# One transformer block on one core: the a weights get a scale of their own, and the a products of the first group run first

## The reference

```python
h = _layernorm(x) * (1 + ca) + sa                 # x: 2 x 4096 x 512
xn = h / norm(h) * sqrt(512) * gamma
q, kv, a = split(xn @ W_qkva.T, 3);  a = sigmoid(a)
y = scan: y[t] = a[t] * y[t-1] + kv[t]            # along the 4096 steps
x = x + ga * (q * y)
h = _layernorm(x) * (1 + cb) + sb                 # then an FFN, whose operands are
x = x + gb * ffn(h)                               # quantised in blocks of 16 to FP4 values
```

## Time and profile before

| | us |
|---|---|
| median of three runs | 1933.85 (1933.53 to 1935.3) |
| the profiled execution's own time | 1935.68 |
| span from its first to its last instruction | 1933.9 |
| PE busy | 1910.6 (99%) |
| DVE busy | 1683.4 (87%) |
| POOL busy | 1298.5 (67%) |
| ACT busy | 759.5 (39%) |
| mean granted TensorE clock | 0.996 |

### The profile page before, as it was taken

The page is one execution under the profiler, slowest core; times in us unless marked ns, Lnnn a source line. Parts: engine busy times, 40 slices in busy tenths (PEclk is TensorE's granted clock), DMA queues, the critical chain, the costliest instruction groups (busy, mean ns, idle before and its releaser), DMA issues.

```text
span 1933.9 us, 26907 instructions
## 1 busy us (share of the span) xinstructions
PE 1910.6 (99%) x9147; PEld 899.7 (47%) x9147; DVE 1683.4 (87%) x2106; ACT 759.5 (39%) x1013; POOL 1298.5 (67%) x1136
## 2 busy tenths in 40 slices
PE   8999999999998999999999999999999999999998
PEld 3344444444444444444444444444444444444444
DVE  7867687778779999999999999999999999999986
ACT  4566767766543233323232323232323322332321
POOL 1568778787767667667766776677667766766641
PEclk9999999999999999999999999999999999999999
DMA  8978788898953433343334333433343343334323
GB/s 292 303 172 217 183 210 207 211 215 185 203 145 90 94 89 73 78 92 86 73 81 96 79 74 84 96 79 74 87 96 73 73 90 93 73 74 93 84 63 78
DMA packets 487300, 234.99 MB, mean 122 GB/s; under 512 B 425906, under 2 KB 425918, under 8 KB 487236
## 3 DMA queue, kind: packets, MB, share of 16 engines
q1 hardware_dynamic: 487236, 234.17, 50.2%
HBM read 95.43 MB, written 33.57 MB: 67 GB/s over the span
## 4 chain that ended last, share of the span: by engine, by line
PE 92%; DVE 3%; POOL 1%; issue 1%; ACT 1%; DMA 1%; SPq 0%; DVEq 0%; POOLq 0%; ACTq 0%
PE bank L1156 45%; PE bank L1085 24%; PE bank L1176 15%; PE bank L1180 7%; PE bank L1024 1%; DMA arena<-in_L_attn_x_dram 0%; DMA arena<-arena 0%; DVE arena L1551 0%; PE bank L1065 0%; PE bank L1192 0%; DVE small L1333 0%; ACT arena L892 0%; POOL arena L691 0%; DVE arena L1491 0%; DVE arena L1464 0%
## 5 line engine op out<-in xcount | busy, mean ns | idle before, releaser
L1156 PE MATMUL bank<-wgu_hi,arena 128*128 128x512 f16 (+1 forms) x3072 | 870.0, 362 | 3.8 <-DVE arena L1491 3.8
L1156 PE MATMUL bank<-wgu_lo,arena 128*128 128x512 f16 (+1 forms) x1536 | 555.6, 362 | 0.0
L1085 PE MATMUL bank<-arena,wq_hi 128*128 128x512 f16 x1536 | 458.1, 380 | 0.0
L1156 PEld LDWEIGHTS bank<-wgu_hi,arena 128*128 128x128 f16 x3072 | 300.8, 98 | 312.7 <-issue 5.5
L1085 PE MATMUL bank<-arena,wq_lo 128*128 128x512 f16 x768 | 291.9, 380 | 0.0
L1176 PE MATMUL bank<-wd_hi,arena 128*128 128x512 f16 x693 | 263.7, 381 | 2.7 <-DMA arena<-arena 2.7
L1176 PE MATMUL bank<-wd_lo,arena 128*128 128x512 f16 x693 | 263.7, 381 | 0.0
L1085 PEld LDWEIGHTS bank<-arena,wq_hi 128*128 128x128 f16 x1536 | 150.3, 98 | 182.2 <-issue 2.7
L1156 PEld LDWEIGHTS bank<-wgu_lo,arena 128*128 128x128 f16 x1536 | 150.4, 98 | 154.2 <-issue 0.6
L720 POOL TENSOR_TENSOR arena<-arena 128x512 f32<-128x512 f32 x63 | 153.1, 2431 | 95.4 <-DVE arena L1566 95.4
L1491 DVE SCALAR_TENSOR_TENSOR arena<-bank,small,arena 128x512 f32<-128x512 f32 (+1 forms) x192 | 134.3, 700 | 86.6 <-PE bank L1156 84.1
(11 more groups left out here) (164 smaller groups left out, 2900.6 us busy)
## 6 DMA issues: line engine op xcount, KB each, us to landing
arena<-in_L_attn_x_dram SPq DMA_DIRECT2D x32, 1024.0 KB, 6.4
arena<-x_scratch SPq DMA_DIRECT2D x128, 256.0 KB, 3.3
x_scratch<-arena SPq DMA_DIRECT2D x16, 1024.0 KB, 8.4
out_dram<-arena SPq DMA_DIRECT2D x64, 256.0 KB, 3.1
arena<-in_L_wmod_dram SPq DMA_DIRECT2D x6, 1024.0 KB, 14.3
arena<-arena SPq DMA_TRANSPOSE x274, 3.5
wgu_hi<-in_L_ffn_w_gate_dram SPq DMA_DIRECT2D x1, 2816.0 KB, 12.1
wgu_lo<-in_L_ffn_w_up_dram SPq DMA_DIRECT2D x1, 2816.0 KB, 19.0
```

The lines of the kernel that those rows point to most:

```text
L1085: last = pe.matmul(dst[:, :].rearrange("p (j t) -> p j t", j=NJ), w[:, k, at], uT[p][:, half, :, k, :], start=(n == 0), stop=(n == 3 * KD ...
L1156: last = pe.matmul(dst[n][:, 0:w], xT[p][:, half, k, :], wt[:, k, cut], start=(m == 0), stop=(m == 3 * KD - 1))
```

## The change

- The a weights (part 2) are scaled by their own maximum and kv and q by theirs. VectorE reduces part 2, the maxima of part 2 and of gamma are turned, put on a diagonal and spread, and `scale_gamma` writes `gamma_a`; the other two parts go through the same steps a second time, behind the low halves of the a tiles, and write `gamma_col` in place. `a_scale` goes to the sigmoids, `qkva_scale` to ga.
- In group 0 TensorE makes all four a products first, with the second pair of maximum steps and `turn_wq(8)` between them; then kv and q of chunks 0 and 1, the FFN rows, kv and q of chunks 2 and 3. Before, each chunk's a stood ahead of its kv and q.
- VectorE multiplies all four tiles of group 0 by one_ca before it adds sa to them, and reduces part 2 behind that. The statistics of group 1 move ahead of the second scale. In group 0 `weight_max(0)` stands ahead of the first `mix`.
- ScalarE copies sa of batch 1 behind the a tiles, makes the first two sigmoids ahead of the other eight tiles, and in group 0 squares behind the third sigmoid.
- SyncE loads the first two modulation parts in two halves each, and x of group 1 behind the transposes of group 0.
- In group 1 TensorE spreads the FFN maxima one product later (behind kv of chunk 2), and VectorE makes their scales behind `weights(1)`, the first steps on the first FFN weight tile.

```diff
         WQ_TILES = [(part, k) for part in (2, 1, 0) for k in range(KD)]
-        WQ_BANKS = [bank[n] for n in (5, 6, 7, 4, 1, 0, 5, 6, 7, 1, 0, 6)]
-        WQ_AFTER = (0, 0, 0, 0, 0, 0, 1, 2, 3, 5, 6, 8)
+        WQ_BANKS = [bank[n] for n in (5, 6, 7, 4, 1, 0, 6, 7, 1, 0, 6, 7)]
+        WQ_AFTER = (0, 0, 0, 0, 0, 0, 2, 3, 5, 6, 7, 8)
...
-                load_modulation(1)
+                load_halves(1)
                 sp.dma_start(xs[0], x_group[0]).then_inc(xs_loaded[0], 16)
-                load_modulation(0)
+                load_halves(0)
...
                 load_modulation(2)
-                sp.dma_start(xs[1], x_group[1]).then_inc(xs_loaded[1], 16)
                 for j in range(NJ):
...
                                  u_half[:, :, j, :].rearrange("p h d -> p (h d)"), transpose=True).then_inc(u0_loaded, 16)
+                sp.dma_start(xs[1], x_group[1]).then_inc(xs_loaded[1], 16)
...
                 act.wait_ge(gamma_scaled, 1)
+                for n in range(KD):
+                    wq_high(n)
+                copy_mix_row(3)
+                copy_ga_row()
                 decays(0, 0)
+                decays(0, 1)
+                act.wait_ge(gamma_scaled, 2)
+                for n in range(KD, NWQ):
+                    wq_high(n)
...
                     if i == 0:
                         apply(1, 1)
-                        decays(0, 1)
-                        squares(1, 1)
                         split_mix(0, 0)
                         decays(0, 2)
+                        squares(1, 1)
+                        split_mix(0, 1)
                         u_hi(1, 1)
+                        decays(0, 3)
                         apply(2, 0)
-                        split_mix(0, 1)
-                        decays(0, 3)
...
                         product_a(0, 0, 0)
-                        for n in range(9, NWQ):
+                        pe.wait_ge(ga_row_copied, 1)
+                        turn_maximum(bank[3], col("part_max", 4)[:, 0:2], max_ready, max_turned, 2, 4)
+                        product_a(0, 0, 1)
+                        spread_maximum(bank[3], max_diagonal, max_all, 2, 2)
+                        product_a(0, 0, 2)
+                        turn_wq(2 * KD)
+                        product_a(0, 0, 3)
+                        for n in range(2 * KD + 1, NWQ):
                             turn_wq(n)
                         turn_ga()
-                        pe.wait_ge(wq_split, 2 * KD)
+                        pe.wait_ge(mix_row_copied, 4)
                         product_kv(0, 0, 0)
...
+                part_maximum(2, 2)
+                diagonal(bank[0], max_turned, max_diagonal, 2)
                 dve.wait_ge(max_all, 1)
+                dve.tensor_copy(col("top_max", 4)[:, 2:4], bank[0][:, P:P + 2]).then_inc(max_copied, 1)
                 dve.wait_ge(max_copied, 1)
+                scale_gamma(col("top_max", 4)[:, 2:3], col("gamma_a", KD))
+                u_lo(0, 0)
+                product_scale(col("a_scale"))
                 dve.wait_ge(gamma_scaled, 1)
+                for n in range(KD):
+                    wq_low(n)
+                part_maximum(0, 1)
+                part_maximum(1, 0)
+                diagonal(bank[3], max_turned, max_diagonal, 2, 2)
+                stats(1, 1)
+                dve.wait_ge(bn_ready, 2 * NJ)
+                mean_var(1, 1)
+                dve.wait_ge(max_all, 2)
+                dve.tensor_copy(col("top_max", 4)[:, 0:2], bank[3][:, P:P + 2]).then_inc(max_copied, 1)
+                dve.wait_ge(max_copied, 2)
+                then(dve.tensor_reduce(col("top_row"), col("top_max", 4)[:, 0:2], AX.X, ALU.max))
+                scale_gamma(col("top_row"), gamma_col)
+                product_scale(col("qkva_scale"))
+                dve.wait_ge(gamma_scaled, 2)
+                for n in range(KD, NWQ):
+                    wq_low(n)
...
                         diagonal(t_bank[0], wmax_turned, wmax_diagonal)
+                    weights(1)
+                    if i == 1:
                         weight_scales()
-                    weights(1)
```

More of the change, by code:

```diff
@@ L202, in adaln_block_kernel @@
         max_turned, max_diagonal, max_copied = sem("max_turned"), sem("max_diagonal"), sem("max_copied")
+        first_half_loaded = [sem(f"wmod{part}_first_half_loaded") for part in range(2)]
         wmax_turned, wmax_diagonal = sem("wmax_turned"), sem("wmax_diagonal")
@@ L1036, in turn_wq, with turn_maximum, spread_maximum @@
                     last.then_inc(wq_turned, 1)
-                def turn_maximum(space, part, ready, turned):
-                    pe.wait_ge(ready, 4)
-                    pe.transpose(space[0:4, 0:P], part, ident[:, :]).then_inc(turned, 1)
-                def spread_maximum(space, diagonal, ready, all_ready):
-                    pe.wait_ge(ready, 1)
-                    pe.matmul(space[:, P:P + 4], ones, diagonal, start=True, stop=True).then_inc(all_ready, 1)
+                def turn_maximum(space, part, ready, turned, n=4, done=4):
+                    pe.wait_ge(ready, done)
+                    pe.transpose(space[0:n, 0:P], part, ident[:, :]).then_inc(turned, 1)
+                def spread_maximum(space, ready, all_ready, n=4, time=1):
+                    pe.wait_ge(ready, time)
+                    pe.matmul(space[:, P:P + n], ones[0:n, :], col("top_diagonal", 4)[0:n, 0:n],
+                              start=True, stop=True).then_inc(all_ready, 1)
                 pe.wait_ge(silu_wide_ready, 1)
@@ L1118, in group @@
                         product_q(0, 0, 0)
-                        product_a(0, 0, 1)
                         pe.wait_ge(ga_copied, 1)
@@ L1293, in _ @@
                     dve.tensor_tensor(u[:, j, :], u[:, j, :], one_ca[:, 0, :], ALU.mult).then_inc(ca0_ready, 1)
+                dve.wait_ge(mix_row_copied, 2)
+                for j in range(NJ):
                     dve.wait_ge(ca0_ready, j + 1)
                     dve.tensor_tensor(u[:, j, :], u[:, j, :], sa[:, 0, :], ALU.add).then_inc(h0_ready, 1)
-                part_maximum(1, 1)
-                part_maximum(2, 0)
-                u_lo(0, 0, (0,))
-                diagonal(bank[3], max_turned, max_diagonal)
```

106 lines of the change are left out of this document (51 added, 55 removed).

## The result

| | before | changed |
|---|---|---|
| median, 8 runs each (us) | 1934.06 (1931.47 to 1935.41) | 1939.94 (1938.45 to 1942.55, and one of 6585.2) |
| ratio of the times | | 1.0029, 95% interval 1.0019 to 1.0039 |
| span of the profiled execution | 1933.9 | 1938.1 |
| mean granted TensorE clock | 0.996 | 0.995 |

The changed kernel is 5.9 us slower by the medians. Forecast were 3.05 us less. (Single runs far out, as 6585, came up for the kernel before too: 2887 in a later series. The one of the kernel before took 1.6 us more than its median, so waits are compared between single executions, and times by the medians.

The account below looks back on a forecast made before the run. TensorE, busy 99% of the span, was taken as the bound, so its start, idle time and clock count. Terms: -2.0 + 1.0 + 0.7 - 2.75 = -3.05 us, giving 1930.8 us, range 1928.2 to 1933.8.

Parts of the forecast that it names:

- So VectorE is 2.2 us later: Group 1: FFN rows start at 58.05 instead of 55.86 us, so VectorE, which sets the pace, runs 2.2 us later.
- the part between the start and group 1: From first product to group 1: +1.0 us for turns and maxima, +0.7 for a new wait; group 1 starts at 78.9.
- the diagonal at 98.83: End of group 1: VectorE's second diagonal step, 1.19 us beside GpSimd's additions, was kept at 1.19.
- The start: Up to TensorE's first product: it starts at 33.9 instead of 35.89 us, -2.0, with the clock falling.
- rival 1: More gain: clock stays up at 24 us (start -2.5), x and VectorE's port early; -4.7 to -5.5; chance 0.2.
- The wait at turn_wq(8): Before group 1: TensorE waits for the fifth low half, needing the second scale and group 1's x; +0.7 us.
- Rival 3: Slower: x of group 1 lands late, delaying kv and q products; +7.7 us and low clock, 1940.4; chance 0.06.
- Group 1: FFN maxima: removes 2.46 us wait and 1.9 of low clock, adds 1.6 of short waits; -2.75 us.
- rival 2: Given back: group 1's two waits lower the clock (+1.9), or group 3 waits for transposes; -1.3, 1932.5; chance 0.2.
- What it gains stays: After 115 us TensorE never waits for 430 us, so its gain carries through to the FFN turn.

Follow-up runs that it names:

- e1: The changed kernel with TensorE's turn of ga earlier and VectorE's ga steps ahead of the last low halves, before GpSimd's additions; 1933.11 us, ratio 0.9996.
- e4: The changed kernel with ScalarE's squares of group 1 moved back ahead of split_mix(0,0); 1935.63 us, ratio 1.0009.
- e2: The changed kernel with GpSimd waiting, before its first addition for group 1, until VectorE finished the ga steps; 1934.03 us, ratio 0.9997.
- e7: The changed kernel with ga steps early, weight_max(0) back behind mix(0,0), and squares ahead of split_mix(0,0); 1932.58 us, ratio 0.9991.
- e10: e7 with TensorE's turn and spread of the FFN maxima each one product later in group 1; 1931.96 us, ratio 0.9991.
- e13: e7 plus two spare matmuls, FFN maxima turned and spread one product later, and x loads ahead of FFN weight transposes; 1931.10 us, ratio 0.9990.
- e6: The kernel before with only the change's group 1 part: FFN maxima spread one product later, scales behind weights(1); 1931.00 us, ratio 0.9986.
- e12: e6 run again, in another series; 1931.64 us, ratio 0.9989.
- e14: e12 with SyncE's x loads issued ahead of the FFN weight transposes; 1931.39 us, ratio 0.9987.
- e9: e7 with two spare matmuls on TensorE ahead of the turn of the maxima at the start; 1932.10 us, ratio 0.9987.

## Why the prediction was wrong

- **The step that failed** is the sentence "So VectorE is 2.2 us later" in group 1, and ahead of it the part between the start and group 1, which gave no time to VectorE's list behind the low halves ("ScalarE's highs and VectorE's lows of the last tiles run beside the fourth a product, and kv's wait for ga is met"). The ga steps were carried over at their old 1.3 us, and measured 6.2. The prediction weighed the shared port of VectorE and GpSimd only for the diagonal at 98.83, not for the steps that the change itself moved beside GpSimd's additions. The moved `weight_max(0)` and squares were not followed to `u_hi`: 8.9 us instead of 2.2 (e1 to e4). Cost on TensorE: a wait of 1.2 at the third FFN row, 3.8 in group 1 and 3.0 of low clock, where the prediction had none of the three.
- **The start**, -2.0 forecast, -0.3 in this profile. Up to the maxima all came within 0.3 us: x at 9.63, additions to 20.5, the maxima at 22.90. I had let the clock fall only from the last modulation row on, for 1.6 us; that row took 6.20 instead of the 5.1 counted, and the small work ahead of it was slow too. In the executions without six spare matmuls in which the clock stayed up the first product came at 33.2 to 33.4: the -2.5 of rival 1. (That rival's -3.6 for group 1 should be -3.45 by its own terms, 2.75 + 0.7.)
- **The wait at turn_wq(8)**, +0.7 forecast: 0.45 here, 1.0 in e1. x of group 1 was no trouble: issued at 31.83, there before VectorE wanted it at 38.95. Rival 3, the only one on the slower side, was wrong; the slower side came from another place.
- **Group 1**: 0.9 us of wait at the turn of the maxima and 0.7 at their spread forecast, with the clock at 1.00. The changed kernel's 0.47 at the spread stands behind a delay of 3.8 us and says little. With the chain mended it was 0.57 and 0.63 in e1, and 0.57 and 1.65 in e2 and e7, there with the low clock that rival 2 had. So the step held in e1 and not in every profile; what was missed is again GpSimd beside `u_lo`.
- **"What it gains stays"**: not all of it. Rival 2 named group 3's transposes; the wait came near 265 us, 1.96 us in e10, behind the round of ScalarE and GpSimd and not behind x loads (e13).
- With the chain mended (e1) the change as forecast gives 1933.11, not 1930.8. The clock at 23 us, a spread that waits 0.63 or 1.65 us, and the wait near 265 may make up for it; the runs don't split the 2.3 us among them.

The Trainium skill (SBUF — State Buffer, "Who interferes with whom") says that of two operations that need the shared port pair the one issued second is blocked until the other ends, and that a reduction never needs it. The trace agrees: the small steps end 0.02 us behind GpSimd's additions, while `weight_max(0)`, with additions beside it, takes 6.02 us for 5632 numbers, in step with the 3.08 for 2816 at 90.85, beside which GpSimd adds nothing.

The best versions by the ratio are the group 1 part alone (e6 0.9986, e12 0.9989, with early x loads e14 0.9987), e9 (0.9987) and e13 (0.9990); the measurements don't tell them apart.

## What to carry to other kernels

Small VectorE steps have no fixed price: when a change moves them, look at what GpSimd does at the new place, since each can cost a whole GpSimd operation (0.17 became 1.0 to 1.3 us here). When an item moves ahead of another in an in-order list, follow the other through every engine that waits for it; three moves, none of which costs much alone, made one chain of 9 us. And a gain at the start of a pipeline is worth only as much as the slack of the next pace, here by the profiles the round between ScalarE and GpSimd. A wait that ends with a DMA (x at 214.8) is not that pace by itself: moving the load (e13) took the wait away and left the product behind it where it was.
